# Down results and addends moved to the GpSimd queue, copies first at the entry of the down stage, and a reordered opening of the second gate/up sweep

## The reference

```python
x = x + _L0_cond_ref(x, ...)          # y = irfft(rfft(u*mask) * rfft(K)) + u*mask*D, times mask
# _L1_cond_ref, with A, B chosen by lora_indices:
gate = lora_add(einsum('bnh,fh->bnf', x, W_gate), x, A_gate, B_gate)
up   = lora_add(einsum('bnh,fh->bnf', x, W_up), x, A_up, B_up)
act  = silu(gate) * up
down = lora_add(einsum('bnf,hf->bnh', act, W_down), act, A_down, B_down)
x = x + down
```

## Time and profile before

| | us |
|---|---|
| three runs | 1740.77, 1743.75, 1743.37 |
| median | 1743.37 |
| the profiled execution | 1738.73 |
| its span, first to last instruction | 1736.7 |

### The profile page before, as it was taken

How to read it: one execution, slowest core, us unless ns; L and a number is a source line. 1 busy time by engine, 2 the same in 40 slices (tenths; PEclk the granted TensorE clock), 3 DMA queues, 4 the chain that set the end, 5 groups by cost and what they waited for, 6 DMA issues and landing times.

```text
span 1736.7 us, 21838 instructions
## 1 busy us (share of the span) xinstructions
PE 1605.6 (92%) x8064; PEld 1369.1 (79%) x8064; DVE 1133.4 (65%) x1604; ACT 628.6 (36%) x828; POOL 114.6 (7%) x185
## 2 busy tenths in 40 slices
PE   2989989999999997899999999996989999889998
PEld 2988878888888886778888888875867887677877
DVE  6544587677767765777777767766556477466574
ACT  2211353333333332543333333335334335343351
POOL 6000022432220000000000000000000000000000
PEclk9999999999999998899999999997999999899999
DMA  8999655786665445234455445548777669688583
GB/s 309 360 327 322 216 191 176 240 262 207 203 203 163 154 152 197 85 110 146 149 158 157 157 153 154 153 139 279 217 247 217 214 215 370 156 255 260 163 271 128
DMA packets 252075, 357.63 MB, mean 206 GB/s; under 512 B 78818, under 2 KB 138018, under 8 KB 251426
## 3 DMA queue, kind: packets, MB, share of 16 engines
q1 hardware_dynamic: 190018, 296.60, 52.5%
q10 hardware_dynamic: 49280, 33.83, 6.7%
q0 software_dynamic: 12672, 25.82, 4.8%
HBM read 276.59 MB, written 105.15 MB: 220 GB/s over the span
## 4 chain that ended last, share of the span: by engine, by line
PE 70%; DMA 11%; DVE 10%; ACTq 3%; issue 3%; ACT 2%; SPq 1%; DVEq 0%
PE ps L995 64%; PE ps L980 6%; DMA out<-res 2%; ACTq L1406 2%; DVE res L1964 2%; DMA tt<-k_pad 2%; DMA y_first<-res 1%; DMA k_pad<-ksb 1%; DMA rraw<-wd 1%; DVE alo L1751 1%; DVE wlo L1751 1%; ACTq L1416 1%; DVE xlo L1751 1%; DMA raw<-a_gu_sel 1%; SPq L857 1%
## 5 line engine op out<-in xcount | busy, mean ns | idle before, releaser
L995 PE MATMUL ps<-xhi,whi 128*128 128x512 f32 (+1 forms) x1080 | 422.1, 391 | 34.7 <-ACT cc L1233 14.5
L995 PE MATMUL ps<-xlo,whi 128*128 128x512 f32 (+1 forms) x1080 | 420.6, 389 | 0.0
L995 PE MATMUL ps<-xhi,wlo 128*128 128x512 f32 (+1 forms) x1080 | 419.2, 388 | 0.0
L995 PE MATMUL ps<-ahi,rhi 128*128 128x512 f32 (+1 forms) x760 | 273.2, 371 | 37.4 <-ACT cc L1233 24.4
L995 PE MATMUL ps<-alo,rhi 128*128 128x512 f32 (+1 forms) x760 | 271.4, 368 | 0.0
L995 PEld LDWEIGHTS ps<-xhi,whi 128*128 128x128 f32 x1080 | 207.1, 192 | 76.1 <-issue 14.9
L995 PEld LDWEIGHTS ps<-xhi,wlo 128*128 128x128 f32 x1080 | 206.5, 191 | 41.4
L995 PEld LDWEIGHTS ps<-xlo,whi 128*128 128x128 f32 x1080 | 207.0, 192 | 37.3
L995 PE MATMUL ps<-ahi,rlo 128*128 128x512 f32 x560 | 222.0, 396 | 0.0
L1233 ACT ACTIVATE rhi<-rraw 128x640 fp32r<-128x640 f32 (+2 forms) x168 | 110.0, 663 | 287.3 <-issue 158.0
L1751 DVE TENSOR_TENSOR rlo<-rraw,rhi 128x640 fp32r<-128x640 f32 x128 | 104.8, 823 | 166.3 <-ACT rhi L1233 166.0
(11 more groups left out here) (182 smaller groups left out, 2034.8 us busy)
## 6 DMA issues: line engine op xcount, KB each, us to landing
raw<-wgu SPq DMA_DIRECT2D x84, 512.0 KB, 5.7
tt<-k_pad SPq DMA_DIRECT2D x64, 512.0 KB, 7.9
araw<-act_sums SPq DMA_DIRECT2D x104, 256.0 KB, 5.6
loraw<-bgu_sel SPq DMA_DIRECT2D x84, 256.0 KB, 4.1
act_keep<-up SPq DMA_DIRECT2D x42, 512.0 KB, 2.8
araw<-act_keep SPq DMA_DIRECT2D x78, 256.0 KB, 4.8
rraw<-wd_sums SPq DMA_DIRECT2D x48, 320.0 KB, 3.5
rraw<-wd SPq DMA_DIRECT2D x36, 320.0 KB, 4.6
```

Of the source, the lines that this page charges most:

```text
L995: return nc.tensor.matmul(out, w, x, start=start, stop=stop, skip_group_check=True)
```

## The change

- `res_in` and `y_store` go, unchanged but for their first wait, from ScalarE's queue to GpSimd's, where `res_in(step)` and `y_store(step)` alternate. `res_in(0)` waits for the first product of the down stage instead of the end of the gate/up stage. With them 64 loads and 64 stores change queues.
- At the entry of the down stage `c1(N-1)` and `v(N-1)` on ScalarE, and `d` and `c2` on VectorE, come earlier among the tiles, and the weights of units 0 to 5 are issued four tiles earlier on SP.
- At the opening of the second sweep `d` goes ahead of `x_form(1, "T1")`; T3, T2 and T4 are formed on GpSimd; B21 gets a place of its own (`c21raw`, in T1's place of `xhi`) and B12's split lies in T2's and T3's places, as in the first sweep; loads, splits and masks are put in another order. `load_pair(FT)` on SP waits for GpSimd's T2, the copy of T1 for its T4, `sums_13(FT)` for its T3.

The diff, cut to its core:

```diff
-        b12hi = place("b12hi", ST, [2 * KB], F32R)
-        b12lo = place("b12lo", S0, [2 * KB], F32R)
+        c21raw = place("c21raw", X0 + 3 * QB, [2 * KB])
...
                 x_again("B12")
+                sp.wait_ge(s_p, prod(FT - 1, "P1"))
+                x_again("B11")
                 wait_lo("lora", FT - 1)
                 load_bl(1)
-                sp.wait_ge(s_p, prod(FT - 1, "P1"))
-                x_again("B11")
-                sp.wait_ge(s_p, prod(FT - 1, "P2"))
+                sp.wait_ge(s_p, prod(FT - 1, "P5"))
                 x_again("B21")
...
                 sp.wait_ge(s_xlo, xsplit(1, "B22"))
+                sp.wait_ge(s_xform, xform(1, "T2"))
                 load_pair(FT)
...
                 sp.wait_ge(s_p, prod(N - 1, p))
-                load_first(*range(7 + 4 * k, 11 + 4 * k))
                 for i in {"P2": (0,), "P7": (1, 2), "P4": (3,), "P3": (4, 5)}.get(p, ()):
                     load_unit(i)
+                load_first(*range(7 + 4 * k, 11 + 4 * k))
...
+            for q, x, y, last in (("T3", "B22", "B12", "P7"), ("T2", "B22", "T1", "P6"), ("T4", "B21", "T2", "P4")):
+                pool.wait_ge(s_p, prod(FT - 1, last))
...
+                nc.gpsimd.tensor_tensor(x_in(1, q), x_in(1, x), x_in(1, y), ALU.subtract).then_inc(s_xform, 1)
+            def res_in(step):
+                u, hp = step // 8, step % 4
+                if step:
+                    pool.wait_ge(s_out, 64 * step)
+                else:
+                    pool.wait_ge(s_dn, 1)
...
+                    if step % 8 < 4:
+                        pool.dma_start(res[:, k, :].rearrange("p (g h n) -> p g h n", g=2, h=HQ), x1_d[:, 2 * j:2 * j + 2, :, c, :]
+                                      ).then_inc(s_res, 16)
+                    else:
+                        pool.dma_start(res[:, k, :], y0_d[:, j, c, :]).then_inc(s_res, 16)
+            def y_store(step):
+                u, hp = step // 8, step % 4
+                pool.wait_ge(s_r, last_result(step))
+                dst = y0_d if step % 8 < 4 else out_d
+                for k, (h, x) in enumerate(RES):
+                    pool.dma_start(dst[:, 2 * u + GRP[x], 2 * hp + h, :], res[:, k, :]).then_inc(s_out, 16)
+            for step in range(DSTEPS):
+                res_in(step)
+                y_store(step)
...
@@ ScalarE
                 v(FT - 1)
+                x_hi(1, "B21")
                 w_hi("wl", 1)
-                x_hi(1, "B21")
+                x_hi(1, "B12")
                 silu(FT - 1)
+                x_hi(1, "B22")
                 w_hi("bl", 1)
-                x_hi(1, "B12")
-                x_hi(1, "B22")
...
                 t_hi(1, "A")
+                w_hi("u0", FT)
                 x_hi(1, "T1")
-                x_hi(1, "T3")
-                w_hi("u0", FT)
-                x_hi(1, "T2")
-                x_hi(1, "T4")
                 t_hi(1, "B")
                 w_hi("u1", FT)
+                x_hi(1, "T3")
+                x_hi(1, "T2")
+                w_hi("u2", FT)
+                x_hi(1, "T4")
                 rest_parts(1, "A")
-                w_hi("u2", FT)
                 rest_parts(1, "B")
             def gu_to_down():
-                for t in ACTS0[:4]:
+                c1(N - 1)
+                for t in ACTS0[:8]:
                     act_hi(*t)
+                v(N - 1)
                 unit_hi(0)
-                c1(N - 1)
-                for t in ACTS0[4:12]:
+                for t in ACTS0[8:12]:
                     act_hi(*t)
                 unit_hi(1)
-                v(N - 1)
...
-            res_in(0)
...
-                    if p == "P2" and step:
-                        y_store(step - 1)
-                    if p == "P5" and step:
-                        res_in(step)
...
@@ VectorE
                 w_lo("agA0", 1)
-                x_form(1, "T1")
                 d(n)
                 w_lo("agA1", 1)
+                x_form(1, "T1")
                 x_lo(1, "B11")
-                x_form(1, "T3")
-                x_form(1, "T2")
-                x_form(1, "T4")
-                w_lo("wl", 1)
                 x_lo(1, "B21")
                 c2(n)
+                w_lo("wl", 1)
                 c12(n)
+                x_lo(1, "B12")
+                mul(n)
+                x_lo(1, "B22")
                 w_lo("bl", 1)
-                mul(n)
-                x_lo(1, "B12")
-                x_lo(1, "B22")
...
             def gu_to_down():
                 n = N - 1
                 for t in ACTS0[:4]:
                     act_lo(*t)
-                unit_lo(0)
+                d(n)
                 for t in ACTS0[4:8]:
                     act_lo(*t)
-                d(n)
+                c2(n)
+                unit_lo(0)
                 for t in ACTS0[8:12]:
                     act_lo(*t)
```

More of the change, by code:

```diff
@@ L539, in x_in @@
         def x_in(u, q):
+            if u and q == "B21":
+                return c21raw[:, :]
             return b12raw[:, :] if q == "B12" else b22raw[:, :] if q == "B22" else xraw[:, QUAD[q], :]
@@ L1021, in lora_a @@
                         q = block_col(x, k)
-                        last = passes(half(ps[4 + i], g), tile(whi, g, k), tile(wlo, g, k), x_tile(u, q, True, k % 4, g),
-                                      x_tile(u, q, False, k % 4, g), k == 0 and g == 0, k == C - 1)
+                        last = passes(half(ps[4 + i], g), tile(whi, g, k), tile(wlo, g, k), x_tile(q, True, k % 4, g),
+                                      x_tile(q, False, k % 4, g), k == 0 and g == 0, k == C - 1)
                     done(last)
@@ L1032, in rest_main @@
                     q = block_col(x, k)
-                    last = passes(ps[6 + i], tile(whi, 2, k), tile(wlo, 2, k), x_tile(u, q, True, k % 4),
-                                  x_tile(u, q, False, k % 4), k == 0)
+                    last = passes(ps[6 + i], tile(whi, 2, k), tile(wlo, 2, k), x_tile(q, True, k % 4),
+                                  x_tile(q, False, k % 4), k == 0)
                 done(last)
@@ L1295, in x_hi @@
                         act.wait_ge(s_x1st, 16 * HQ)
-                    if u == 0 and q in ("T3", "T2"):
-                        act.wait_ge(s_p, pro(0, 6))
+                    if q in ("T3", "T2"):
+                        act.wait_ge(s_p, pro(u, 6))
+                    if u and q == "T1":
+                        act.wait_ge(s_xform, xform(1, "T4"))
+                        act.wait_ge(s_xlo, xsplit(1, "B21"))
                 elif q == "B22":
@@ L1303, in x_hi @@
                     if q == "B12":
-                        act.wait_ge(s_ast[0], stored(FT - 1))
+                        act.wait_ge(s_p, prod(FT - 1, "P6"))
                     else:
                         act.wait_ge(s_p, prod(FT - 1, "P1" if q == "B11" else "P2"))
-                copy(part_of(x_split(u, q, True), part), x_source(u, q, part)).then_inc(s_xhi, 1)
+                copy(part_of(x_split(q, True), part), x_source(u, q, part)).then_inc(s_xhi, 1)
             def t_hi(u, x):
@@ L1393, in y_v @@
                 copy(v2[:, :], banks(0)["P6"]).then_inc(s_yv, 1)
-            def res_in(step):
-                u, hp = step // 8, step % 4
-                if step:
-                    act.wait_ge(s_out, 64 * step)
-                else:
-                    act.wait_ge(s_p, END_GU)
-                    act.wait_ge(s_ast[1], stored(N - 2))
-                    act.wait_ge(s_tq, 4 * 20)
-                for k, (h, x) in enumerate(RES):
-                    j, c = 2 * u + GRP[x], 2 * hp + h
-                    if step % 8 < 4:
-                        act.dma_start(res[:, k, :].rearrange("p (g h n) -> p g h n", g=2, h=HQ), x1_d[:, 2 * j:2 * j + 2, :, c, :]
-                                      ).then_inc(s_res, 16)
-                    else:
-                        act.dma_start(res[:, k, :], y0_d[:, j, c, :]).then_inc(s_res, 16)
-            def y_store(step):
-                u, hp = step // 8, step % 4
-                act.wait_ge(s_r, last_result(step))
-                dst = y0_d if step % 8 < 4 else out_d
-                for k, (h, x) in enumerate(RES):
-                    act.dma_start(dst[:, 2 * u + GRP[x], 2 * hp + h, :], res[:, k, :]).then_inc(s_out, 16)
             def td_parts(u):
@@ L1533, in _ @@
                     silu(N - 1)
-            y_store(DSTEPS - 1)
-            act.wait_ge(s_out, 64 * DSTEPS)
         @block.vector
@@ L1823, in x_lo @@
                 if u:
-                    dve.wait_ge(s_xform, xform(u, {"B11": "T1", "B21": "T4", "B12": "T3", "B22": "T2",
-                                                   "T1": "T2", "T3": "T3", "T2": "T4", "T4": "T4"}[q]))
+                    dve.wait_ge(s_xform, xform(u, {"T1": "T2", "T3": "T3", "T2": "T4", "T4": "T4"}.get(q, "T1")))
                 elif q in TS:
@@ L1830, in x_lo @@
                     dve.wait_ge(s_cev, HH * (HQ - 1) if part == "pre" else H)
-                sub(part_of(x_split(u, q, False), part), x_source(u, q, part),
```

(10 more changed lines are left out.)

32 lines of the change are left out of this document (21 added, 11 removed).

## The result

| | before | after |
|---|---|---|
| median of 4 runs, us | 1742.07 | 1719.52 |
| lowest and highest | 1735.37 to 1743.75 | 1715.29 to 1721.52 |
| profiled execution | 1738.73 | 1721.52 |
| its span | 1736.7 | 1719.8 |

The changed kernel is faster by 22.5 us: ratio 0.9874, 95% interval 0.9842 to 0.9907. The forecast was 1696, 47 us faster: the direction and the range held, the gain was a little under half of the forecast one.

What follows compares the result with a forecast made beforehand. The kernel was taken as bound by matmuls (TensorE busy 92%), with only holes and lower-clock time to regain. 12 + 8 + 27 = 47 us off 1743.4 gives 1696 (itself 1684 to 1712); range 1682 to 1727.

Steps and rivals of the forecast that it cites:

- the landing of the addends' loads: Down stage: the four loads of addends issued on GpSimd land 4 us behind their issue.
- the chain: Down stage: last addition, stores, landing, loads, landing, y_sums, next last addition: 27.8 us against TensorE's 23.8 a step.
- covered: Down stage: no chain hole into steps 3 and 11 (start 2.7 us after P1), nor in 5 to 7, 13 to 15.
- Part 1: Opening of the second sweep: d(20) ahead of T1's form, first lolo ending at 735.2 instead of 747.2; 12 us gained.
- I take it as hidden: Opening: three forms on GpSimd, at most 7.5 us each, are ready in time and cost nothing.
- rival B: Opening: GpSimd's forms and VectorE's subtractions exclude each other; 7 us taken as lost, 1703 us; chance 0.20.
- Part 2: Entry of the down stage: c1 at 1165.3, P6 starting at 1203.5 instead of 1211.1; 8 us gained.
- Part 3: Down stage: 64 stores and 64 loads leave ScalarE's queue; 41 us less 10.4, 2.8 and 1 makes 27 gained.
- the clock term: Down stage: 10 us of lower-clock losses behind five holes go with those holes.
- A: Down stage: the addends' chain binds in all x_keep steps, 4 us more per chain; 1716 to 1730 us; chance 0.16.
- C: Down stage: GpSimd takes 2 us for each of its 128 DMAs, so the kernel is slower, 1766 us; chance 0.08.
- D: Whole kernel: the chain never binds and forms are free, 12 + 10 + 41, 1680 us; chance 0.07.

Runs made afterwards that it cites:

- the kernel with copies: All of the change, but GpSimd's three subtractions (T3, T2, T4) are one-input copies, so the result is wrong; 1708.76 us in a single run.
- sums late: All of the change, but in the down stage the sums are added into res at P3 instead of P6; 1704.63 us, ratio 0.9782.
- step 3 in rows: Down step 3 of the changed kernel with first halves' addends read in 2 KB rows instead of 256-byte pieces (wrong elements); 1708.72 us, ratio 0.9789.

## Why the prediction was half right

Two steps of the prediction failed. It took the forms moved to GpSimd as hidden, and they held three VectorE instructions up by 10.8 us, 8.4 us of the opening. And it took 4 us for the landing of the addends' loads, which was 7.1 in step 3 and 6.6 to 8.8 in nine of the ten steps in which VectorE waits for it; with that the chain held VectorE in steps that had been taken as covered.

**What bounds it, and in which direction.** Right. The holes were the right ones, those ended by cc went but for one of 3.4 us in step 8, and the time fell.

**Part 1, forecast 12, measured 4.0 in the trace, and 2.3 with the clock.** d(20) ahead of the form, P4 at once, a hole before lora_a: all as told. The step that failed is "I take it as hidden". The upper end of 7.5 us for a form was looked at only for when its result is needed, and for that it was fine (the forms took 6.60, 6.43 and 4.82). That VectorE stands still meanwhile was given to rival B at 0.20. B was the case: the three operations took 10.8 us more than normal. Its price, 7 us, was near too: after gained 8.4 us less than the kernel with copies (72.9 against 64.5). The rest of the queue's sum was right, 12 forecast and 12.4 in the kernel in which GpSimd's work is short.

A term that stood at nothing is the clock behind the longer hole ahead of the first lolo: 1.7 us, and that hole and the lower clock behind it are there with the forms on VectorE as well (5.4 us, clock 0.52) and with copies (5.8 us, 0.70).

The hold-up is the rule of the Trainium skill (SBUF — State Buffer, "Who interferes with whom") that the prediction named against itself; the trace agrees with it where the kernel touches it: instructions with two SBUF inputs wait for the whole of GpSimd's (5.62 us for 2.29), and VectorE's 1.21 us on one PSUM and one SBUF input go undisturbed. GPSIMD Engine Reference, "Elementwise — side-by-side cycle accounting", a page of the Trainium skill, gives 4.5 us for a form; the trace has 4.4 for the part that ran alone.

**Part 2, forecast 8, measured 5.7.** The size is near by luck, the reason was wrong for the most part. The forecast gave it to the order of copies and weights; the experiments give 3 to 4.5 of it to the four loads that left ScalarE's queue, which stood in no term of part 2. The row for that was at hand: ScalarE needed 6.20 us for four loads in step 2, and 7.22 at the entry itself; with the new order and the DMA engines full, two of them alone took 12.5.

**Part 3, forecast 27, measured 12.4 less 2.5 at the end, 10.** The terms one by one:

| term | forecast | after | sums late |
|---|---|---|---|
| idle time taken from TensorE | 31 - 7.2 - 1.8 = 22 | 11.3 | 25.0 |
| busy time (clock) | 10 - 3.2 - 1 = 5.8 | 2.1 | 8.2 |
| end of the kernel | -1 | -2.5 | -2.6 |

(From the entry of P6, so with 0.9 us that the table of stretches counts at the entry; late sums: idle 33.8 to 8.8, busy 484.2 to 476.0.) The chain was the right suspect, and it binds at steps 4 and 12 with 4.1 and 4.7 us where 3.6 was forecast. The mis-sized term is the landing of the loads:

| | forecast | step 3 after | step 3 in rows |
|---|---|---|---|
| stores, to the last landing | 8.6 | 8.7 | 9.75 |
| issue of four loads | 4.5 | 3.5 | 2.1 |
| landing behind it | 4 | 7.1 | 5.4 |
| last addition to sums | 17 | 19.4 | 17.3 |
| sums to last addition | 10.7 | 10.1 | |
| period (TensorE's step 23.8) | 27.8 | 29.4 | |

The page's median of 6.9 us from issue to landing was read as holding only while four are in the queue; the trace has 7.1 behind the last of the four. Step 3 is one case of it: the chain from the stores to the sums took 20.7, 19.4, 19.8 and 18.5 us in steps 2, 3, 10 and 11, where 17 were forecast, so there are holes of 2.3 and 1.5 us ahead of P1 of steps 3 and 11 that the forecast took as covered. The loads in rows of steps 5 to 7 and 13 to 15 were "covered" too; they make VectorE wait in all six steps (0.6 to 6.9 us), and TensorE 1.9 and 2.3 us at the tails of steps 5 and 7. Most of these holes brought a lower clock again, 0.50 to 0.66 in the 5 us behind those ahead of P1 of steps 3, 4 and 12, at the tail of step 5 and in step 8 (1308.8 to 1313.8 ran at 0.50, 1.2 GHz), so most of the 10 us of clock behind the old holes were not gained. That the clock term as such was sound is shown by the late sums, 8.2 of 10.

**The rivals.** A (the chain, 0.16) and B (the forms, 0.20) were priced as if only one could come. They are in different stages and hang on nothing common. B came whole, A in part: the chain makes holes at four of the seven steps that A names. After the fact B's 8 us and the 17 us that the down stage lacked are 25 of 47, which leaves 22 where 22.5 were measured; the forecast had no such case. C fell: a load in pieces takes GpSimd 0.9 us. D, for which the forms had to be free and the chain never to bind, fell with both.

**What the text named as signs.** "Wrong if TensorE's holes in the down stage sum to over 20 us": 22.5. "Wrong if y_sums waits over 5 us in most steps": it waits in 10 of 16, and over 5 us in seven, so this sign stayed just short. "Cc never the releaser of TensorE": it still is, once in the stage, 3.4 us in step 8. VectorE subtractions over 2.3 us for B: 5.62.

## What to carry to other kernels

An instruction that moves to GpSimd is not off VectorE if both work on SBUF: count GpSimd's duration into VectorE's queue wherever VectorE has two SBUF inputs, and move the work only into VectorE's idle time or beside its instructions that read PSUM and one SBUF tile. When a wait leaves one queue, ask what stands behind it in the next: here the stores and loads stopped holding ScalarE, and their landing then held VectorE, until the waiting addition was put two products later in its queue, an edit that gains nothing by itself. When waits are gathered into one longer hole, look at the granted clock behind it. Price independent rivals together, not only each alone.

## What the runs showed of the hardware

- VectorE (two inputs in SBUF) and GpSimd (reading SBUF, with one input or two) exclude each other for whole instructions, in both directions: 5.62 us for 2.29, 3.81 for 0.69, 5.59 for 1.22 beside subtractions that need some 4.4 us for themselves, and the same to 0.02 us in five traces; 2.98, 1.13, 2.90 beside copies that need some 1.8. VectorE with one input in PSUM and one in SBUF is not held: 1.21 us in the middle of a subtraction.
- ScalarE was held for long by issuing a load of 1024 pieces of 256 bytes while the DMA engines were full: 6.67 and 5.80 us for each of two, at 358 to 388 GB/s, where the two ahead of them took 0.40 and 0.60. On GpSimd the same load took 0.9 us at 389 GB/s.
- The same 64 loads and 64 stores make fewer packets from GpSimd: in the page's part on queues ScalarE's q10 goes from 49280 packets to 2176 and GpSimd's q0 from 12672 to 22912. After:

```profile
q0 software_dynamic: 22912, 59.39, 10.9%
...
q10 hardware_dynamic: 2176, 0.26, 0.1%
```

- The stores of the last step take longer to the end from GpSimd: from the start of the last matmul to the end 7.9 to 8.0 us with the stores on ScalarE (three traces), 10.2 to 10.6 on GpSimd (nine).
- Open: why that is so, and how much of the 7.1 us of landing is other traffic; neither was tried.
